# A lift shared between two engines: GpSimd takes 6 of 25 source tiles while VectorE searches the maximum, and VectorE reads the rows of maxima where TensorE left them

## The reference

```python
h = (x @ W).reshape(N, H, C)
al_s = jnp.einsum('nhc,hc->nh', h, a_src)
al_d = jnp.einsum('nhc,hc->nh', h, a_dst)
e = jax.nn.leaky_relu(al_s[src] + al_d[dst], 0.2)
m = jax.ops.segment_max(e, dst, num_segments=N)
ex = jnp.exp(e - m[dst])
denom = jax.ops.segment_sum(ex, dst, num_segments=N)
out = jax.ops.segment_sum(h[src] * (ex / denom[dst])[:, :, None], dst, num_segments=N)
```

## Time and profile before

| what | value |
|---|---|
| median of three runs | 4488.0 us |
| the profiled execution | 4485.12 us |
| its span on the core | 4483.3 us |
| busy: PE, DVE, ACT, POOL | 3600.2, 2860.0, 2241.0, 708.7 us |
| mean granted TensorE clock | 0.882 |
| first attention, first lift to last weigh | 2032.1 to about 3456 us |
| second attention, first lift to last weigh | 3690.6 to about 4060 us |
| the chain at the start, until X is read | 0 to 56.9 us |

### The profile page before, as it was taken

One profiled execution on the slowest core, in us unless ns is written; L12 is line 12 of the kernel. 1 busy time (PEld: TensorE's weight loads), 2 busy tenths in 40 slices (PEclk: granted clock), 3 DMA queues, 4 the chain that ended last, 5 costly groups with the idle time before them and its releaser, 6 DMA issues. The chain is left out here.

```text
span 4483.3 us, 70197 instructions
## 1 busy us (share of the span) xinstructions
PE 3600.2 (80%) x21308; PEld 2884.0 (64%) x21309; DVE 2860.0 (64%) x6577; ACT 2241.0 (50%) x5503; POOL 708.7 (16%) x491
## 2 busy tenths in 40 slices
PE   4766999989869999836999999899899268886391
PEld 3333555568768999825777777777778257775160
DVE  6877887811141000239999999999997529996312
ACT  4981367820033444325666666666665457763030
POOL 2991000000023000400111111111110000000404
PEclk9557999999969999958999999999999689996595
DMA  4970234554231111231111111111100323321223
GB/s 121 221 174 13 88 146 177 232 220 147 99 110 45 55 55 55 74 142 35 44 43 43 43 43 43 43 43 43 38 32 39 134 92 107 106 91 39 78 76 107
DMA packets 100401, 396.61 MB, mean 88 GB/s; under 512 B 11870, under 2 KB 56386, under 8 KB 77266
## 3 DMA queue, kind: packets, MB, share of 16 engines
q1 hardware_dynamic: 82940, 344.48, 22.3%
q0 software_dynamic: 14976, 44.58, 3.2%
q10 hardware_dynamic: 2368, 6.03, 0.6%
HBM read 270.45 MB, written 124.59 MB: 88 GB/s over the span
## 5 line engine op out<-in xcount | busy, mean ns | idle before, releaser
L1298 PE MATMUL gat_agg<-f_XN,gat_A 128*128 128x257 f32 x5000 | 1132.8, 385 | 22.1 <-DVE gat_A L1403 22.1
L1298 PEld LDWEIGHTS gat_agg<-f_XN,gat_A 128*128 128x128 f32 x5000 | 956.0, 193 | 163.2 <-DVE gat_A L1403 22.7
L1232 ACT ACTIVATE kept_X<-kept_X,gat_s 128x128 f32<-128x128 f32 x2500 | 741.4, 387 | 481.5 <-DVE kept_X L1392 481.5
L1392 DVE SCALAR_TENSOR_TENSOR kept_X<-gat_r,gat_s 128x128 f32<-128x128 f32 x2500 | 664.9, 345 | 45.8 <-POOL gat_r L1180 45.7
L2312 ACT ACTIVATE moe_exp_h<-moe_exp_hbank,moe_b1c 128x128 f32<-128x128 f32 x742 | 271.3, 367 | 541.1 <-PE moe_exp_hbank L2263 364.8
L868 PE MATMUL mat_cw<-mat_join,mat_lane 128*128 128x400 f16 x2976 | 509.8, 334 | 35.1 <-issue 19.2
L868 PEld LDWEIGHTS mat_cw<-mat_join,mat_lane 128*128 128x128 f16 x2976 | 290.7, 98 | 254.7 <-issue 48.1
L1365 DVE CUSTOM_DVE_ANT_0 gat_junk<-gat_als,gat_absT 128x3200 bf16<-128x3200 f32 x100 | 348.1, 3481 | 25.4 <-DMA gat_als<-score_rows 16.5
L2270 PE MATMUL moe_exp_ybank<-moe_exp_w2b,moe_exp_h 128*128 128x256 f32 x1484 | 350.0, 384 | 9.5 <-DVE kept_X L2332 3.4
L1403 DVE SCALAR_TENSOR_TENSOR gat_A<-kept_X,gat_C 128x1664 f32<-128x1664 f32 x200 | 354.1, 1812 | 0.0
L2346 DVE TENSOR_TENSOR moe_exp_xgT<-moe_exp_ybank,moe_b 128x256 f32 x109 | 46.3, 425 | 460.0 <-PE moe_exp_ybank L2270 460.0
(11 more groups left out here) (369 smaller groups left out, 4699.7 us busy)
## 6 DMA issues: line engine op xcount, KB each, us to landing
gat_C<-count_matrix SPq DMA_DIRECT2D x50, 1600.0 KB, 6.5
count_matrix<-mat_both SPq DMA_DIRECT2D x25, 1600.0 KB, 5.3
weight_matrix<-mat_both SPq DMA_DIRECT2D x25, 1600.0 KB, 8.8
edge_raw<-in_edge_attr_dram SPq DMA_DIRECT2D x50, 768.0 KB, 6.1
e_WT<-weight_matrix SPq DMA_DIRECT2D x13, 1600.0 KB, 6.6
sum_more<-weight_matrix SPq DMA_DIRECT2D x12, 1600.0 KB, 6.6
slot_rows<-moe_exp_xgT POOLq DMA_DIRECT2D x22, 640.0 KB, 3.7
hidden<-gat_h1t SPq DMA_DIRECT2D x25, 512.0 KB, 2.8
```

What stands on the lines that cost most here:

```text
L1232: last = nc.scalar.activation(w, w, ACT.Exp, bias=s02[:, t, h:h + 1])
L1298: last = nc.tensor.matmul(agg[h % 2][:, 0:D + 1], A[h % 2][:, t, :], g.XN[:, t, :], start=(t == 0), stop=(t == NT - 1))
L1392: last = nc.vector.scalar_tensor_tensor(out=work[h % 2][:, t * P:(t + 1) * P], in0=r1[:, h, :], scalar=s08[:, t, h:h + 1], in1=r2[:, h, :] ...
```

## The change

It has four parts.

1. **The lift is shared.** `POOL_TILES = 6`: of the 25 source tiles of a lift the last six go to GpSimd, for heads 1 to 3 in the first attention and for every tile in the second. GpSimd (`share`) does it in seven instructions: six `tensor_scalar` of 128 columns, max(r3 + 0.8 x source score, 0), and one `tensor_tensor` over 768 columns that adds r2. The row r3 = 0.8 x destination score is made by ACT (`steep_rows`, `steep_row`). ACT's second half of the exponentials waits for GpSimd's share as well.
2. **The rows are made by DVE from the bank.** `keep_max` on ACT and `rows` on GpSimd are gone. DVE's new `rows` makes r1 and r2 in two instructions with the bank `mrow` as an operand. In the first attention it stands at h = 3, behind `top(i+2, 0)` and ahead of the lift; in the second as `rows(i+2)` between `add_output(i-2)` and `weigh(i)`.
3. **No diagonal.** PE spreads the maximum by a product with the maxima themselves as the stationary operand, repeated over 128 columns, and the identity as the moving one; `m_diag` is gone. In the first attention four products of 128 columns take the place of one of 512, and they stand in the middle of head 1, no longer behind it.
4. **The start.** SP issues the load of the 24 full tiles of X behind the two reads of the shifted destinations (`prev`, `nxt`), no longer ahead of them.

```diff
@@ prepare, sync
-            sp.dma_start(X[:, 0:NT - 1, :], a["x"][0:full, :].rearrange("(t p) d -> p t d", p=P)).then_inc(g.x_in, 16)
...
             sp.dma_start(nxt, g.dpad[2:2 + E_PAD].rearrange("(r w) -> r w", w=EW)).then_inc(spread, 16)
+            sp.dma_start(X[:, 0:NT - 1, :], a["x"][0:full, :].rearrange("(t p) d -> p t d", p=P)).then_inc(g.x_in, 16)
@@ gat_heads, gpsimd
+            def share(i, h):
+                if h == 1:
+                    wait_alone(pool, r_ready, i * 2 + 2)
+                    wait_alone(pool, r3_ready, i + 1)
+                if not (starts(i) and h < 2):
+                    wait_alone(pool, A_ready, (i * UN + h) * 2 - 2)
+                for t in range(NT - POOL_TILES, NT):
+                    last = nc.gpsimd.tensor_scalar(work[h % 2][:, t * P:(t + 1) * P], r3[:, h, :], s08[:, t, h:h + 1], 0.0,
+                                                   ALU.add, ALU.max)
+                last.then_inc(raised, 1)
+                wait_alone(pool, raised, i * (UN - 1) + h)
+                mine = work[h % 2][:, (NT - POOL_TILES) * P:NT * P].rearrange("p (t d) -> p t d", d=P)
+                nc.gpsimd.tensor_tensor(mine, mine, r2[:, h, :].rearrange("p (o d) -> p o d", o=1)
+                                        .to_broadcast([P, POOL_TILES, P]), ALU.add).then_inc(share_ready, 1)
@@ gat_heads, scalar
+                    if part == 1 and h > 0:
+                        act.wait_ge(share_ready, i * (UN - 1) + h)
...
+            def steep_rows(i):
+
+                wait_alone(act, c_in, i * 32 + 32)
+                if not starts(i):
+                    wait_alone(act, share_ready, i * (UN - 1))
+                nc.scalar.activation(r3[:, :, :], ar[:, at(i % 2), :, :].rearrange("p o h d -> p (o h) d"), ACT.Copy,
+                                     scale=1.0 - SLOPE1).then_inc(r3_ready, 1)
@@ gat_heads, tensor
-                nc.tensor.matmul(mrow[:, 0:H1 * P], g.ones[:, :], m_diag[:, :, :].rearrange("p h d -> p (h d)"),
-                                 start=True, stop=True).then_inc(mrow_ready, 1)
+                for h in range(H1):
+                    last = nc.tensor.matmul(mrow[:, h * P:(h + 1) * P], m[:, h:h + 1].to_broadcast([P, P]), g.ident[:, :],
+                                            start=True, stop=True)
+                last.then_inc(mrow_ready, 1)
@@ gat_heads, vector
+            def rows(i):
+
+                mine = ar[:, at(i % 2), :, :].rearrange("p o h d -> p (o h d)")
+                top_row = mrow[:, 0:H1 * P]
+                dve.wait_ge(mrow_ready, i + 1)
+                dve.wait_ge(r3_ready, i + 1)
                 if not starts(i):
+                    dve.wait_ge(share_ready, i * (UN - 1))
+                nc.vector.tensor_tensor(r1[:, :, :].rearrange("p h d -> p (h d)"), mine, top_row,
+                                        ALU.subtract).then_inc(r_ready, 1)
+                nc.vector.scalar_tensor_tensor(out=r2[:, :, :].rearrange("p h d -> p (h d)"), in0=mine, scalar=SLOPE1,
+                                               in1=top_row, op0=ALU.mult, op1=ALU.subtract).then_inc(r_ready, 1)
...
-                    for t in range(half.start, half.stop):
+                    for t in range(half.start, min(half.stop, NT if h == 0 else NT - POOL_TILES)):
...
+                    if h == 3 and not near_end(i, 1):
+                        rows(i + 1)
@@ gat_single, vector
+            def rows(i, b):
+                mine = ar[:, slot(i), :].rearrange("p o d -> p (o d)")
+                dve.wait_ge(mrow_ready, i + 1)
+                if not (isinstance(i, int) and i < 2):
+                    dve.wait_ge(share_ready, i - 1)
+                nc.vector.tensor_tensor(r1[:, b, :], mine, mrow[:, 0:P], ALU.subtract).then_inc(r_ready, 1)
+                nc.vector.scalar_tensor_tensor(out=r2[:, b, :], in0=mine, scalar=SLOPE1, in1=mrow[:, 0:P],
+                                               op0=ALU.mult, op1=ALU.subtract).then_inc(r_ready, 1)
...
                     add_output(i - 2, b)
+                if not near_end(i, 2):
+                    rows(i + 2, b)
                 weigh(i, b)
```

More of the change, by code:

```diff
@@ L1167, in _, with body @@
         def _(pool):
[L1169 to L1183 removed]
+            def share(i, h):
[12 more added lines that the diff above has]
+                                        .to_broadcast([P, POOL_TILES, P]), ALU.add).then_inc(share_ready, 1)
+            def body(i):
+                for h in range(1, H1):
+                    share(i, h)
+            pool.wait_ge(scaled_s, 1)
+            pool.wait_ge(x_out, 16)
+            body(0)
             with pool.Fori(1, NT) as i:
[L1185 removed]
+                body(i)
         @block.scalar
@@ L1218, in absents @@
                                      scale=-BIG, bias=g.big[:, 0:1]).then_inc(absent_ready, 1)
-            def keep_max(i):
-                act.wait_ge(mrow_ready, i + 1)
-                if not starts(i):
-                    act.wait_ge(r_ready, i * 2)
-                nc.scalar.activation(m_row[:, :, :].rearrange("p h d -> p (h d)"), mrow[:, 0:H1 * P],
-                                     ACT.Copy).then_inc(mrow_kept, 1)
             def exps(i, h):
@@ L1253, in body @@
                         exps(ni, nh)
+                    if h == 2 and not near_end(i, 1):
+                        steep_rows(i + 1)
                     ends(i, h)
@@ L1326, in times_w1, with between @@
                 last.then_inc(out_ready, 1)
+            def between(i):
+                if not near_end(i, 2):
+                    turn_absent(i + 2)
+                if not near_end(i, 1):
+                    spread_max(i + 1)
             def body(i):
@@ L1330, in body @@
                 for h in range(H1):
-                    head(i, h, first and h < 2,
-                         (lambda: turn_absent(i + 2)) if h == 1 and not near_end(i, 2) else None)
-                    if h == 1 and not near_end(i, 1):
-                        spread_max(i + 1)
+                    head(i, h, first and h < 2, (lambda: between(i)) if h == 1 else None)
                     if h >= 1:
@@ L1449, in _ @@
             dve.wait_ge(x_out, 16)
+            rows(0)
             lift(0, 0)
@@ L1717, in absents @@
                                      scale=-BIG, bias=g.big[:, 0:1]).then_inc(absent_ready, 1)
-            def keep_max(i):
-                act.wait_ge(mrow_ready, i + 1)
-                if not (isinstance(i, int) and i == 0):
-                    act.wait_ge(r_ready, i * 2)
-                nc.scalar.activation(m_row[:, :], mrow[:, 0:P], ACT.Copy).then_inc(mrow_kept, 1)
             def exps(i, b):
@@ L1737, in body, with steep_row @@
                 if not near_end(i, 2):
-                    keep_max(i + 2)
+                    steep_row(i + 2, b)
                 if not near_end(i, 4):
                     absents(i + 4)
-            absents(0)
-            absents(1)
-            keep_max(0)
-            absents(2)
-            keep_max(1)
-            absents(3)
+            def steep_row(i, b):
+                wait_alone(act, c_in, i * 32 + 32)
+                if not (isinstance(i, int) and i < 2):
+                    wait_alone(act, share_ready, i - 1)
+                nc.scalar.activation(r3[:, b, :], ar[:, slot(i), :].rearrange("p o d -> p (o d)"), ACT.Copy,
+                                     scale=1.0 - SLOPE1).then_inc(r3_ready, 1)
+            for i in range(4):
+                absents(i)
+                if i < 2:
+                    steep_row(i, i)
             act.wait_ge(scaled_s, 1)
@@ L1808, in top @@
                 dve.wait_ge(step, i * PER + 1)
+                if not (isinstance(i, int) and i == 0):
+                    dve.wait_ge(mrow_ready, i)
                 nc.vector.tensor_tensor(m[:, :], mx[:, :], g.AL[:, at(i), 1], ALU.add).then_inc(step, 1)
@@ L1822, in lift @@
                 for half in halves:
-                    for t in range(half.start, half.stop):
+                    for t in range(half.start, min(half.stop, NT - POOL_TILES)):
                         last = nc.vector.scalar_tensor_tensor(out=work[b][:, t * P:(t + 1) * P], in0=r1[:, b, :],
@@ L1868, in _ @@
             dve.wait_ge(scaled_s, 1)
+            rows(0, 0)
+            rows(1, 1)
             lift(0, 0)
```

111 lines of the change are left out of this document (41 added, 70 removed).

## The result

The kernel after takes 4500.9 us (median of 17 runs, 4497.95 to 4503.69) against 4487.5 us (17 runs, 4482.67 to 4497.52) on the same chips: ratio 1.0030, 95% interval 1.0022 to 1.0037, so 0.3% slower and clear of noise. The prediction was 4398 us, range 4345 to 4468, with 0.09 for slower. It was wrong in size and in sign.

The account below looks back on a forecast made before the run. DVE was taken to set the pace, with PE close behind in the first attention. First attention -113, second +29, start -6 gave -90 from 4485.1: 4395, or 4398 us as median; range 4345 to 4468.

Parts of the forecast that it names:

- the price of the six `tensor_scalar`: First attention, GpSimd: 0.31 us each, 1.9 us for six, so its share would cost DVE 0.8 us a tile.
- the coupling to PE: First attention: with DVE at 52 us and PE at 51.1, any hiccup of PE delays DVE; 0.5 us a tile added.
- The rule of the lock: DVE and GpSimd exclude each other: GpSimd's share is free beside the maximum and costs DVE its excess beside a lift.
- the third rival: First attention: a dear tensor_scalar makes the kernel slower, all share beyond 3.4 us being DVE's; 4619 us at 0.8; chance 0.10.
- The ring in the second attention: DVE's rows wait 1.5 us for PE's spreading, delaying the weigh PE needs: turn 15.7 us against 15.2.
- The clock: Second attention, PE: a lower-clock piece costs 1.7 us, taken every second turn: +0.8, period 16.5 us, +29 us in all.
- The rows and the wait that goes: First attention, DVE: two new row instructions cost 1.2 us a tile; the 1.8 us wait before head 0's lift ends.
- The margin of 0.3 us: First attention: ACT's r3 is ready at 11.7 us, DVE reaches rows at 12.0, so no wait was taken.
- The start: Before the attentions: destinations land at 11 us in place of 21.91; -6 us taken, bounds -11 and -3.
- The other forecast for this place: At the start: prev and nxt, behind X, land at about 38 us and DVE, wanting them at 32, waits 6.

Follow-up runs that it names:

- E1: Kernel after, with GpSimd's tensor_scalar adding the constant 0.5 in place of the source score read through a pointer: 4496.5 us, one run.
- E2: Kernel after, with GpSimd's add of r2 over 768 columns left out in both attentions: 4390.6 us, ratio 0.9776 to the kernel before.
- E3: Kernel after, with GpSimd's add of 768 columns replaced by a one-input tensor_scalar over the same columns, in both attentions: 4429.3 us, one run.
- E6: Kernel after, with GpSimd's six additions in a scratch buffer before its wait, and the second attention's spreading in mid-head: 4357.3 us, ratio 0.9718.
- E9: E6 with ScalarE making the steep row before the exponentials in the second attention: 4328.3 us, ratio 0.9643 to the kernel before.
- E4: Kernel after, with PE's spreading of the maximum moved from behind the head into its middle, second attention alone: 4467.8 us, ratio 0.9952.
- E8: Kernel after, with eight unread products filling PE's wait in every turn of the second attention: 4474.1 us, one run.

## Why the prediction was wrong

**The step that failed** is the price of the six `tensor_scalar` in the first attention: "I take 0.31, since it reads one tensor as the cast does: 1.9 us", with 0.456 as the upper bound from the earlier trace rows. They take 4.16 us, 0.69 each. The bounds came from rows of another form: a cast and a two-input subtraction, neither with two operations in one instruction. E1 shows that the form costs 0.64 even with constants. With 0.31 the add ends 0.3 to 0.7 us behind the maximum, with 0.69 it starts behind it, and so the whole 1.84 us fall beside the lift. Three adds of 1.6 to 1.8 are 5.1 us a tile in place of 0.8. That is 4.3 x 24 = 103 us, and the first attention missed its forecast by 113 - 20 = 93; most of the other 10 are the 0.5 a tile that I had added for the coupling to PE and that didn't come. The rest of the estimate held: 51.3 + 5.1 = 56.4 against 56.5 measured; E2, which takes the add away, has 51.8.

**The rule of the lock** was half right. The long instruction costs VectorE its own length less 0.27 us (1.57 of the add's 1.84, 0.58 of E3's 0.85), so the forecast's "costs DVE its excess beside a lift" nearly holds for the add. It doesn't for the short ones, as E6's lift of 5.28 us beside four to five of them and E9's of 5.27 beside all six show. This is why the third rival, which would have put the break-even at a `tensor_scalar` of 0.53 us, overstates. At 0.69 its share is 0.25 + 4.16 + 0.3 + 1.84 = 6.55 us, an excess over 3.4 of 3.2 a head, and it is 1.7. That is the excess of 5.0 a tile that the rival gave as its turning point (worked out without the 0.5 for the coupling, which the same rival's sum for 0.8 us counts, and which didn't come), and the first attention gained 20 us, nearly the 23 named there to pay for the rest. The rest cost 39.8 - 2.5 = 37.3, and so the sum is a loss of 17. The outcome is this rival at its threshold, to which I had given 0.10.

**The ring in the second attention** was right: a wait of L1842 of 1.5 us in each turn, PE's wait of 2.6, the slower turn. E4, which takes the spreading off the ring, ends the wait of L1842 and the slower turn; PE's wait falls in every second turn only (2.46 and 1.25 in turn), as VectorE then sets the pace. The clock was mis-sized. I took every second turn for a piece of low clock, and gave 17.4 us as the bound with one in each; there is one in each, and the turn is 17.1. That is +39.8 for +29. E8, where the turn falls to 15.7 at the higher clock, shows that the clock's part is real.

**The rows and the wait that goes**: 2 x 0.60 us on VectorE for the 1.2 forecast, the 1.80 gone, and no wait for ScalarE's r3. The margin of 0.3 us sufficed.

**The start**: -4.5 by the layer norm for the -6 taken, as the destinations land at 17.4 and not at 11, though X no longer shares their queues. The other forecast for this place, that VectorE would wait some 6 us for `prev` and `nxt` held by X, didn't come: L328 starts 21.3 us after the cast in both kernels. Of the 4.5, 2.5 reach the first attention.

## What to carry over

Price an instruction only from a row of the same form on the same engine. Where none is there, let the range reach to where the step's arithmetic changes kind: here the point at which the add slips from beside the maximum to beside the lift, which is worth 5 us a tile. When work goes to an engine that can block another, list which of its instructions block and place those, and only those, in the other's uncontended stretch; the rest can be done whenever its inputs exist, into a buffer of its own. The same change, with the same instructions, went from 0.3% slower to 3.6% faster by where GpSimd's share, PE's spreading and ScalarE's steep row stand. A smaller share than six tiles, which would also end sooner, was not run. And an instruction that waits in an in-order queue ahead of the bottleneck's work makes a ring: look for its producer's place in the other queue before it is moved.
